# Four graph layers on one core: the loops of indirect edge gathers and attribute scatters written out

## The reference, cut to what matters

```
L0: msg = h_rel[etype, src] * norm;  out = segment_sum(msg, dst) + bias     (32 relations from 8 bases)
L1: two graph convolutions with self-loops and degree scaling, relu between
L2: s, v = hs[src], hv[src] of the edges (idx_i = src, idx_j = dst in the call);
    messages from edge_attr_20, edge_attr_4 and edge_weight, summed per node
L3: two SAGE convolutions, tanh between
```

## Time and profile before

| | us |
|---|---|
| Median of three runs | 2274.22 (2269.99 to 2284.41) |
| Span of the profiled execution, first to last instruction | 2029.4 |
| Whole time of the profiled execution | not given on the page |
| Edge gathers, first to last start | 70.5 to 522.8 |
| Attribute scatters, first to last start | 591.7 to 1090.5 |
| Message gathers, first to last start | 1196.8 to 1628.9 |

### The profile page before, as it was taken

One profiled execution on the slowest core, in us unless ns is written; L12 is line 12 of the kernel. 1 busy time (PEld: TensorE's weight loads), 2 busy tenths in 40 slices (PEclk: granted clock), 3 DMA queues, 4 the chain that ended last, 5 costly groups with the idle time before them and its releaser, 6 DMA issues.

```text
span 2029.4 us, 26409 instructions
## 1 busy us (share of the span) xinstructions
PE 1663.5 (82%) x6615; PEld 978.4 (48%) x6615; DVE 1049.0 (52%) x2893; ACT 350.3 (17%) x781; POOL 1037.0 (51%) x1300
## 2 busy tenths in 40 slices
PE   0577777787789999929999877888887765999999
PEld 0566666666433333415545354444444444544543
DVE  8466566566567777782010337877877734001001
ACT  2100000000000000021110144444444356011000
POOL 5477677677236766767773037777777710000000
PEclk9999999999989989969999958888889966999999
DMA  4666666666632332220001022222222320001001
GB/s 143 176 181 182 175 184 182 181 182 181 185 93 72 92 114 76 72 96 18 23 22 24 0 89 67 62 66 62 66 61 66 54 11 1 0 0 42 0 11 40
DMA packets 109823, 170.07 MB, mean 84 GB/s; under 512 B 42193, under 2 KB 64902, under 8 KB 109774
## 3 DMA queue, kind: packets, MB, share of 16 engines
q0 software_dynamic: 45808, 109.25, 20.2%
q1 hardware_dynamic: 47662, 32.12, 5.5%
q10 hardware_dynamic: 16304, 28.05, 4.6%
HBM read 151.64 MB, written 17.70 MB: 83 GB/s over the span
## 4 chain that ended last, share of the span: by engine, by line
PE 45%; issue 18%; POOL 16%; DMA 7%; DVE 6%; ACT 6%; POOLq 1%; DVEq 0%; SPq 0%; ACTq 0%
PE ps L846 17%; PE ps L784 10%; PE ps L857 10%; POOL u L695 8%; POOL gath L620 7%; DMA gath<-h_rows,idx 5%; PE ps L928 2%; PE ps L733 2%; DVE ident L1031 1%; PE ps L769 1%; ACT hs L417 1%; PE ps L907 1%; DMA u<-u_rows,at 1%; PE ps L894 1%; ACT L570 1%
## 5 line engine op out<-in xcount | busy, mean ns | idle before, releaser
L733 PE MATMUL ps<-spread,gath 128*128 128x128 f32 x2504 | 361.5, 289 | 98.1 <-DMA gath<-h_rows,idx 92.9
L695 POOL DMA_INDIRECT u<-u_rows,at x336 | 331.0, 985 | 205.3 <-DMA u_rows<-u 103.2
L665 POOL DMA_INDIRECT slots<-att,idx_s x313 | 318.1, 1016 | 139.1 <-issue 76.4
L733 PEld LDWEIGHTS ps<-spread,gath 128*128 128x128 f32 x2504 | 306.5, 193 | 153.0 <-issue 96.5
L620 POOL DMA_INDIRECT gath<-h_rows,idx x313 | 302.6, 967 | 135.5 <-issue 71.4
L846 PE MATMUL ps<-adj,hs 128*128 128x417 f32 (+1 forms) x960 | 338.4, 514 | 23.6 <-DVE adj L1310 23.6
L784 PE MATMUL ps<-base_t,z 128*128 128x512 f32 (+1 forms) x640 | 317.9, 619 | 10.0 <-DMA base_t<-in_bases_dram 6.6
L1109 DVE TENSOR_TENSOR z<-z,ps 128x512 f32 x313 | 214.9, 687 | 133.1 <-PE ps L733 131.5
L846 PEld LDWEIGHTS ps<-adj,hs 128*128 128x128 f32 x960 | 181.9, 190 | 178.4 <-issue 154.6
L928 PE MATMUL ps<-msg,hot 128*128 128x256 f32 x672 | 197.3, 445 | 69.6 <-DVE msg L1408 69.6
L928 PEld LDWEIGHTS ps<-msg,hot 128*128 128x128 f32 x672 | 142.2, 221 | 138.0 <-issue 95.8
(11 more groups left out here) (199 smaller groups left out, 1592.0 us busy)
## 6 DMA issues: line engine op xcount, KB each, us to landing
base_t<-in_bases_dram ACTq DMA_DIRECT2D x64, 256.0 KB
slots<-zero_t SPq DMA_DIRECT2D x6, 896.0 KB, 5.5
at<-slots SPq DMA_DIRECT2D x21, 256.0 KB
u<-u_rows,at POOLq DMA_INDIRECT x336, 2.5
et_i<-in_etype_dram SPq DMA_DIRECT2D x40, 128.0 KB, 4.8
att<-in_attr_dram SPq DMA_DIRECT2D x79, 64.0 KB
gath<-h_rows,idx POOLq DMA_INDIRECT x313, 3.6
slots<-att,idx_s POOLq DMA_INDIRECT x313
```

The lines of the kernel that those rows point to most:

```text
L665: nc.gpsimd.indirect_dma_start(out=slots, out_offset=bass.IndirectOffsetOnAxis(ap=idx_s[0:r, par, c:c + 1], axis=0), in_=att[0:r, par, c, ...
L695: nc.gpsimd.indirect_dma_start(out=u[:, s8 % QUAD, c, :], out_offset=None, in_=u_rows, in_offset=bass.IndirectOffsetOnAxis(ap=at_i[:, c, D ...
L733: last = mm(bank[:, k * P:(k + 1) * P], gath[:, h_slot, k * P:(k + 1) * P], s_of.rearrange("p b d -> p (b d)"), start=True, stop=True)
```

## The change

On GpSimd, both loops are written out by the program that builds the kernel: 313 gathers and 313 scatters stand one after another in the code, each with constants as wait values. Because each instruction now knows its column, the gather reads its index from `src_i` and the scatter from `slot_i` in place. The copies into `idx` and `idx_s`, and the semaphores `idx_ok` and `att_ok`, go. The scatter loop waits once per quad, for the attribute load.

The two words that GpSimd used to write into the attribute rows are laid there by the host: word 25 is `dst` and word 26 is the whole of `src`, both as integer bits. VectorE takes the low seven bits when it fills `src_of`, which becomes an integer tile.

```
-            def gather_ring(i, par, skip, chunks=RING):
-                for c in range(chunks):
-                    if c % QUAD == 0:
-                        nc.gpsimd.tensor_copy(idx[:, 2 * par + c // QUAD, :],
-                                              src_i[:, bass.ds(i * 2 * RING + par * RING + c, QUAD)]).then_inc(idx_ok, 1)
-                    indexed = in_reg(pool, i * 4 + 2 * par + c // QUAD + 1)
-                    used = in_reg(pool, i * 2 * RING + par * RING + c - RING + 1)
-                    pool.wait_ge(fit_ok, 1)
-                    if not skip:
-                        pool.wait_ge(z_pe, used)
-                    pool.wait_ge(idx_ok, indexed)
-                    nc.gpsimd.indirect_dma_start(... idx[:, 2 * par + c // QUAD, c % QUAD:c % QUAD + 1] ...)
...
+                for c in range(REAL_CHUNKS):
+                    if c >= RING:
+                        pool.wait_ge(z_pe, c - RING + 1)
                     nc.gpsimd.indirect_dma_start(
+                        out=gath[:, c % RING, :], out_offset=None, in_=h_rows,
+                        in_offset=bass.IndirectOffsetOnAxis(ap=src_i[:, c:c + 1], axis=0)).then_inc(gathered[c % RING], 16)
...
-            def scatter_quad(g, par, lap, tail):
-                ...
-                nc.gpsimd.tensor_copy(at_i[:, :, DSTC:DSTC + 1], dst_i[:, bass.ds(g * QUAD, QUAD)].unsqueeze(2))
-                nc.gpsimd.tensor_copy(att[:, par, :, SRCC:SRCC + 1], srclo[:, bass.ds(g * QUAD, QUAD)].unsqueeze(2))
-                nc.gpsimd.tensor_copy(idx_s[:, par, :], slot_i[:, bass.ds(g * QUAD, QUAD)]).then_inc(att_ok, 1)
...
+            for c in range(REAL_CHUNKS):
+                par, lap = c // QUAD % 2, c // (2 * QUAD)
+                if c % QUAD == 0:
+                    pool.wait_ge(ld_att[par], lap * 16 + 16)
+                r = TAIL if c == REAL_CHUNKS - 1 else P
+                nc.gpsimd.indirect_dma_start(
+                    out=slots, out_offset=bass.IndirectOffsetOnAxis(ap=slot_i[0:r, c:c + 1], axis=0),
+                    in_=att[0:r, par, c % QUAD, :], in_offset=None).then_inc(st_att[par], 16)
...
-                    v.tensor_copy(src_of[:, rpar, :, :], slot_words(rpar, SRCC, SRCC + 1))
+                    v.tensor_scalar(src_of[:, rpar, :, :], slot_words(rpar, SRCC, SRCC + 1).bitcast(i32), P - 1, None,
+                                    ALU.bitwise_and)
...
     words = [np.asarray(edge_attr_20), np.asarray(edge_attr_4), np.asarray(edge_weight).reshape(EDGES, 1),
-             np.zeros((EDGES, ROW - RCUT - 1), f32)]
+             np.asarray(dst, np.int32).reshape(EDGES, 1).view(f32), np.asarray(src, np.int32).reshape(EDGES, 1).view(f32),
+             np.zeros((EDGES, ROW - SRCC - 1), f32)]
```

More of the change, by code:

```diff
@@ L108, in graph_layers @@
         start_k = sb(ctx, "start_k", [P, BLOCKS + 1], f32)
-        idx_s = sb(ctx, "idx_s", [P, 2, QUAD], i32)
         stat6 = sb(ctx, "stat6", [P, BLOCKS, 6], f32)
@@ L146, in graph_layers @@
         gath = sb(part, "gath", [P, RING, FEAT], f32)
-        idx = sb(part, "idx", [P, 4, QUAD], i32)
+        idx = sb(part, "idx", [P, 1], i32)
         spread = sb(part, "spread", [P, 2, QUAD, BASES, WIN], f32)
@@ L196, in graph_layers @@
         yr = sb(late, "yr", [P, 2, QUAD * QUAD, 4], f32)
-        src_of = sb(late, "src_of", [P, 2, QUAD * QUAD, 1], f32)
+        src_of = sb(late, "src_of", [P, 2, QUAD * QUAD, 1], i32)
         at_t = sb(late, "at_t", [P, QUAD * P], f32)
@@ L239, in graph_layers @@
         ln_stat, ln_std, ln_rs, ln_h = semaphores("ln_stat ln_std ln_rs ln_h")
-        idx_ok, spread_ok, z_pe, z_add = semaphores("idx_ok spread_ok z_pe z_add")
+        spread_ok, z_pe, z_add = semaphores("spread_ok z_pe z_add")
         g_idx, g_gath, g_spread, g_pe, g_add, edges_done = semaphores(
@@ L606, in _ @@
             pool.wait_ge(coef_ok, SLICES)
-            def gather_ring(i, par, skip, chunks=RING):
-                for c in range(chunks):
-                    if c % QUAD == 0:
-                        nc.gpsimd.tensor_copy(idx[:, 2 * par + c // QUAD, :],
-                                              src_i[:, bass.ds(i * 2 * RING + par * RING + c, QUAD)]).then_inc(idx_ok, 1)
-                    indexed = in_reg(pool, i * 4 + 2 * par + c // QUAD + 1)
-                    used = in_reg(pool, i * 2 * RING + par * RING + c - RING + 1)
-                    pool.wait_ge(fit_ok, 1)
-                    if not skip:
-                        pool.wait_ge(z_pe, used)
-                    pool.wait_ge(idx_ok, indexed)
-                    nc.gpsimd.indirect_dma_start(
[L621 to L632, removed]
+            with pool.If(pool.value_load(fits[0:1, 0:1], min_val=0, max_val=1) == 1):
+                for c in range(REAL_CHUNKS):
+                    if c >= RING:
+                        pool.wait_ge(z_pe, c - RING + 1)
+                    nc.gpsimd.indirect_dma_start(
+                        out=gath[:, c % RING, :], out_offset=None, in_=h_rows,
+                        in_offset=bass.IndirectOffsetOnAxis(ap=src_i[:, c:c + 1], axis=0)).then_inc(gathered[c % RING], 16)
             with pool.Else():
@@ L637, in _ @@
                     pool.wait_ge(g_add, used)
-                    nc.gpsimd.tensor_copy(idx[:, 0, 0:1], src_i[:, bass.ds(c, 1)]).then_inc(g_idx, 1)
+                    nc.gpsimd.tensor_copy(idx[:, 0:1], src_i[:, bass.ds(c, 1)]).then_inc(g_idx, 1)
                     indexed = in_reg(pool, c + 1)
```

22 lines of the change are left out of this document (2 added, 20 removed).

## The result

The changed kernel takes 2587.01 us (median of four, 2575.38 to 2588.21) against 2278.27 us (2269.99 to 2284.41) for the kernel before on the same chip. The ratio is 1.135 [1.131, 1.138]: slower by 13%, where 2221 us were forecast.

What follows compares the result with a forecast made beforehand. It took GpSimd to pace the edge stage and TensorE the count stage. Span 2029.4 less 53.4 us from the edge gathers, other parts at nothing, plus 244.8 around it, made 2221 us, range 2207 to 2246.

Steps and rivals of the forecast that it cites:

- Part 1: Edge stage: without index copies and their waits, the gathers' pitch falls from 1.450 to about 1.28 us, gaining 53.4 us.
- the two odd stalls: Edge gathers: two gaps of 2.22 and 0.85 us that no index copy explains, kept in the forecast as 2.5 us.
- Part 2: Scatters beside the counts: three copies and one index wait per quad go, scatters end near 960 us; costed at nothing.
- those 103 us: After the last scatter: GpSimd's idle wait of 103.2 us for u_rows, taken as cover for the scatters.
- Part 3: VectorE's src_of edit and integer comparison in the message stage: 7 us at most, hidden behind GpSimd's gathers.
- The sum: Whole kernel: span 2029.4 - 53.4 = 1976.0 us, with 244.8 us around it unchanged, makes 2221 us.
- Rival A: Edge stage: TensorE or the gathers' landing becomes the bound at 1.36 us each; gain 28, 2246 us; chance 0.10.
- Rival B: Edge stage: transfers already bound it, or hidden register or semaphore work keeps the pitch; 2274 us; chance 0.08.
- Rival C: GpSimd waits for its own straight-line code, 82 us lost against 53 gained; 2303 us; chance 0.05.
- Rival D: More than forecast: 60 us, odd stalls vanish, a few us in the count stage; some 65 us, 2209 us; chance 0.05.

Runs made afterwards that it cites:

- scatter_same_ops: Kernel before with only the scatter loop written out, all copies and waits kept; 2276.29 us, 0.989 of before on chip 15 (B).
- scatter_ahead: Kernel before, scatter loop kept, host words instead of two word copies, index copied a quad ahead; 2607.73 us, 1.136 of before on chip 15 (B).
- behind_third: Changed kernel, each scatter waiting for three times as many counts; 0.969 of before on chip 11 (A), 1.074 on chip 10 (B).
- behind_sparse: Changed kernel, each scatter waiting for four times as many counts; 1990.23 us, 0.981 of before on chip 14 (A).

## Why the prediction was wrong, point by point

**Part 1, the edge gathers: right on A, wrong on the chip of the record.** On A the stage went from 452.3 to 391.5 us, 60.8 us less, at a pitch of 1.255. The forecast was 53.4 with 60 as its best bound. The difference is the gathers' mean, 948 to 950 ns instead of the 967 that I kept, and the two odd stalls, which vanished. Every gap is 0.30; the changed kernel on chip 13:

```profile
228.02 0.95 POOL L610 DMA_INDIRECT gath<-h_rows,src_i  x1 [0.30 <-PE ps L698]
229.27 0.94 POOL L610 DMA_INDIRECT gath<-h_rows,src_i  x1 [0.30 <-issue]
230.52 0.95 POOL L610 DMA_INDIRECT gath<-h_rows,src_i  x1 [0.30 <-PE ps L698]
```

The same kernel in the stretch of the earlier trace rows:

```profile
178.00:232.00 54.00, 48.95 (x346) 41.80 (x347) 37.70 (x66) 0.00 (x0) 40.89 (x44) 1.00 0.73 209
```

The DMA engines' share of 0.73 was forecast, and it makes 0.73 x 1.255 = 0.92 us per gather. The 2.0 us estimated from the table of the Trainium skill, "DMA: Bandwidth & Descriptors", section "Measured (HBM→SBUF, 128 partitions, SWDGE, issued from GpSimd)", do not hold for these rows. On the record's own chip the stage took 470 us (before, chip 3: 479), which is above the 430 that the prediction named as its failure. There the ring holds the gathers, not GpSimd; the changed kernel on the record:

```profile
409.04 0.22 DVE L1059 TENSOR_TENSOR hit<-iota_w,offs 128x64 f32<-128x64 f32 x1
...
415.32 0.69 DVE L1074 TENSOR_TENSOR z<-z,ps 128x512 f32 x1 [6.06 <-remote]
```

So of the 61 us only 9 are left on B. The raw records point to what VectorE waited for in this hole: the signal, not the product. TensorE's matmuls for the addition at 415.32 end at 408.3 us by their records (modelled ends), but semaphore updates for them are recorded at 403.1 and then three within 0.2 us from 415.2 on, and GpSimd's next gather, which waits on the same semaphore, starts right after too. Of the 305 recorded updates of that semaphore in the edge stage 134 come within 0.15 us of the one before; on chip 13 none of 313 do. Why they come late in bursts was not found.

**Part 2, the scatters: the step that failed.** The prediction says: "I cost this part at nothing; its cover is those 103 us", and "That the copies stop disturbing VectorE in this stage I cost at nothing as well, TensorE being busy through". The cover was there: on A the last scatter went out at 951 us (forecast: near 960) and the wait for `u_rows` grew to 183.2 us (forecast: 180), all as worked out. But cover hides a part's own time, not what it does to the others. On B the scatters that I made denser, one per 1.39 us instead of 1.60, multiplied VectorE's sequencer time per count by six (0.5 to 3.2 us) and cost some 300 us in the counts, which are on the path. I had no term for it, and none of my rivals was of this kind: none had the scatters slow another engine. The experiments place it at the scatters' rhythm: scatter_same_ops against scatter_ahead, and behind_third. The cover itself was also less free than I said: behind_sparse shows that SyncE's weight loads wait behind the scatters before GpSimd's cover runs out.

**Part 3, VectorE: right.** The comparison with an integer operand costs nothing; the changed kernel on the record:

```profile
L1359 DVE TENSOR_TENSOR hot<-iota_h,src_of x84: 677/684/708, 1606.2 to 2196.6; 128x512 f32<-128x512 f32 x84
```

**The sum: a second error.** "I put the difference of the median to the span [...] 244.8 us, around it" was wrong: 1.8 us lie around a span. 11% between a trace and the runs that it stands for should have been read as two conditions of the chip. The missing time of the kernel before on B lies in the stages: edge +26, counts +79, message gathers +153 (chip 3 against the trace shown), 258 of the 262 us between the spans. Had I seen this, I would have known only that the trace was no picture of the runs, which is reason enough for a far wider range. The range's upper end is mis-added as well: 2236 + 7 + 8 is 2251 and not 2246, which changes nothing here.

**The rivals.** Rival A, TensorE as the bound at 1.36, did not come on group A, where the pitch is 1.255. On B its sign did, gathers waiting for L698 (36.0 us, and 66.2 of "remote"), at a pitch of 1.506; TensorE itself, with 365 busy of 470 us, was not the bound. Rival B fell on group A; on B the outcome is near it, for another reason. Rival C, GpSimd waiting for code: its gaps stay at 0.30, and scatter_same_ops loses nothing (0.989). The Trainium skill, "Runtime: NRT & Kernel Launch", section "Instruction fetch mechanics", says that code is fetched ahead in sequence; both agree with it. Rival D named the right numbers for group A, 60 us and the odd stalls; its few us from the count stage did not come (275 and 274 us). Slower came, by a way that I did not name.

## What to carry to other kernels

Before a part is costed at nothing, ask not only what hides it but what runs beside it and how its rhythm changes: removing pauses from a stream of indirect scatters that nothing waits for cost 13% on one group of chips. When a trace's span and the median of the runs differ by more than a few us, find the stage in which they differ before forecasting. And what gained 3% on one chip lost 13% on another: measure on several before keeping such a change.

## What the hardware showed that I had not expected

- Two groups of chips: the same kernel takes 2030 us on chips 7, 11, 13 and 14 and 2221 to 2298 us on 3, 10 and 15. Within B they differ too (2221 on chip 10). What sets the groups apart stays open.
- On group B, beside dense scatters of 128 rows of 128 bytes, the median register, branch or semaphore instruction of VectorE and SyncE takes 0.70 us instead of 0.04, and 84 of TensorE's matmuls stood 133.2 us in "issue", up to 2.6 each. Beside the gathers on B, one per 1.51 us, no sequencer instruction of VectorE lasts over 0.5 us from 100 to 500 us; what is late there are semaphore updates. On group A neither is seen (0 of VectorE's 1076 over 0.5 us). What the queues share with the transfers was not found.
- The Trainium skill, "SBUF — State Buffer", section "SBUF: two separate sides", holds that a DMA and a compute operation cannot slow each other there. For the operations themselves the traces agree: a count's mean is 320 ns beside the stream on the record and 319 in the kernel before on chip 3. The slowing lies between them, of which the section says nothing.
- The message stage, whose code on GpSimd did not change, takes 579 to 604 us on B and 429 to 433 on A, in either kernel, with VectorE's sequencer median at 0.04 us. In the kernel before, GpSimd's gathers there wait 156.9 us for VectorE's messages (L1408) on chip 3 and 1.2 on the trace shown. The cause was not looked into.
